# 1444-key attention: maxima as 32-row passes on quarters of the array, full-array products in front of the scores, three maxima in every key tile

## The reference

```python
qm, km, vm = (split_heads(t) for t in (q @ Wq.T + bq, k @ Wk.T + bk, v @ Wv.T + bv))
scores = einsum('bnlh,bnph->bnlp', qm, km) / sqrt(8)
scores = where(mask, scores, -1e8)
attn = softmax(scores, axis=-1)
out = einsum('bnlp,bnph->bnlh', attn, vm) @ Wo.T + bo
x = x + tanh(g_xattn[1]) * out
```

## Time and profile before

| what | value |
|---|---|
| median of 3 runs | 2146.14 us (2143.47 to 2155.18) |
| profiled execution, its own time | 2144.45 us |
| its span | 2142.7 us |
| mean granted clock of PE | 0.933 |
| PE busy | 89% of the span |
| VectorE, ScalarE, POOL busy | 69%, 62%, 31% |

### The profile page before, as it was taken

The page is one execution under the profiler, slowest core; times in us unless marked ns, Lnnn a source line. Parts: engine busy times, 40 slices in busy tenths (PEclk is TensorE's granted clock), DMA queues, the critical chain, the costliest instruction groups (busy, mean ns, idle before and its releaser), DMA issues. The chain is left out here.

```text
span 2142.7 us, 42902 instructions
## 1 busy us (share of the span) xinstructions
PE 1912.9 (89%) x16792; PEld 1207.6 (56%) x16792; DVE 1481.6 (69%) x3509; ACT 1323.4 (62%) x2169; POOL 670.7 (31%) x605
## 2 busy tenths in 40 slices
PE   3669999766899999999999999999999779999997
PEld 2536666544455656656565665656666445555553
DVE  4845666686677787877878787787884476677541
ACT  2645667677056766666676676766767355666643
POOL 1420233321421222322222222222210323565666
PEclk9879999867689999999999999999999597999998
DMA  5025555101232323323233232322322202212222
GB/s 159 1 68 176 186 168 186 36 20 39 85 120 74 133 83 111 115 83 133 77 117 106 92 132 67 127 96 101 129 77 67 63 15 47 50 36 36 36 71 43
DMA packets 126293, 190.74 MB, mean 89 GB/s; under 512 B 42018, under 2 KB 99466, under 8 KB 125710
## 3 DMA queue, kind: packets, MB, share of 16 engines
q1 hardware_dynamic: 126094, 188.01, 28.3%
HBM read 104.84 MB, written 11.76 MB: 54 GB/s over the span
## 5 line engine op out<-in xcount | busy, mean ns | idle before, releaser
L1608 DVE TENSOR_REDUCE b_part_max<-psum 128x1 f32<-128x482 f32 (+3 forms) x1248 | 741.7, 651 | 214.8 <-PE psum L1494 198.7
L1414 ACT ACTIVATE b_PT<-psum 128x800 f32<-128x800 f32 x768 | 608.2, 836 | 227.8 <-PE psum L1513 220.9
L1494 PE MATMUL psum<-b_KH,b_QBD 64*128 64x482 f32 (+1 forms) x1152 | 417.4, 438 | 21.2 <-DVE b_part_max L1608 18.5
L1513 PE MATMUL psum<-b_QS,b_KS 64*128 64x200 f32 x3072 | 420.4, 285 | 0.3 <-ACT b_PT L1414 0.3
L1513 PEld LDWEIGHTS psum<-b_QS,b_KS 64*128 64x128 f32 x3072 | 340.1, 187 | 5.7 <-ACT b_PT L1414 4.6
L1529 PE MATMUL psum<-b_PT,b_V 128*32 128x200 f32 x6144 | 341.5, 340 | 0.4 <-ACT b_PT L1414 0.4
L1339 POOL TENSOR_TENSOR b_KL<-b_KF,b_KH 128x1444 fp32r<-128x1444 f32 x32 | 107.0, 3342 | 589.0 <-PE psum L1513 565.7
L1494 PEld LDWEIGHTS psum<-b_KH,b_QBD 64*128 64x128 f32 x1152 | 194.2, 189 | 165.0 <-DVE b_part_max L1608 88.5
L1529 PEld LDWEIGHTS psum<-b_PT,b_V 128*32 128x32 f32 x6144 | 160.0, 109 | 144.1 <-ACT b_PT L1414 78.7
L1815 POOL TENSOR_TENSOR c_HE<-c_HE,c_G 128x400 f32<-128x400 f32 x128 | 131.6, 1032 | 115.1 <-ACT c_HE L1961 113.9
L426 POOL TENSOR_TENSOR a_rs<-a_ve,a_half 100x4 f32<-100x4 f32 x48 | 48.5, 1011 | 311.8 <-DVE a_ve L918 311.7
(11 more groups left out here) (280 smaller groups left out, 2996.2 us busy)
## 6 DMA issues: line engine op xcount, KB each, us to landing
b_KS<-b_KH SPq DMA_DIRECT2D x64, 722.0 KB
a_CT<-in_ctxt SPq DMA_DIRECT2D x32, 722.0 KB, 5.6
b_CT<-in_ctxt SPq DMA_DIRECT2D x32, 722.0 KB, 4.2
b_KS<-b_KL SPq DMA_DIRECT2D x32, 722.0 KB
a_CN<-in_ctxn SPq DMA_DIRECT2D x32, 704.0 KB
c_G<-gates_scratch SPq DMA_DIRECT2D x16, 800.0 KB, 4.3
att_scratch<-b_AO SPq DMA_DIRECT2D x32, 200.0 KB, 5.8
b_MB<-in_mask SPq DMA_DIRECT2D x32, 180.5 KB, 4.3
```

Source lines behind the costliest of these rows:

```text
L1414: nc.scalar.activation(PT[:, kt % 2, 2 * a:2 * a + 2, :], psum[:, 2 * a:2 * a + 2, 0:TG], ACT.Exp).then_inc(sem["pt_ready"], 1)
L1494: m = mm(bank(b, D, size), QBD[rows, j % 2, tile * D:(tile + 1) * D], KH[rows, j % 2, at_:at_ + size], start=True, stop=True)
L1513: m = mm(bank(p, D, 2 * T, (s % 2) * 2 * T), KS[rows, j % 2, s, kt * D:(kt + 1) * D], QS[rows, j % 2, s * 2 * T:(s + 1) * 2 * T], start=Tr ...
L1608: v.tensor_reduce(part_max[0:rows, n % 2, q, c:c + 1], bank(b, rows, CHUNKS[c][1]), AX.X, ALU.max)\
```

## The change

Each half of the array becomes two quarters of 32 rows. The columns of the projection weights are ordered so that a quarter holds four whole heads. `QBD` shrinks from 800 to 400 columns, and each quarter has 400 rows of maxima: three tiles of 128 and 16 left. A main maximum is now a pass of 32 rows by 128 columns, with the tile position given. The left-over rows of the four quarters are again one 64-column pass of 128 rows. The count of passes stays 36 + 3.

Each key tile has three maxima: one upper and two lower in even tiles, two upper and one lower in odd ones. Upper ones stand before score pieces 0 and 2, lower ones before piece 3, two in succession where there are two. Successive maxima of one half go to its two quarters in turn.

The jobs on the full array (query, key, value, left-over maxima) move from behind the scores to in front of them (`FRONT`); the turn stays behind (`BEHIND`). The left-over maxima stand in tiles 2, 6 and 7 instead of 5, 6 and 7, and the last main maximum is the last of all. The new order of rows asks for more transfers: 13 for `KS` and 10 for the maxima's rows of `QS`. ScalarE drains the values one tile earlier in its own order.

```diff
-TILES_ROW = 6
-LEFT = 32
-MAXES = 2 * TILES_ROW * 3 + 3
+QUARTERS, QROW, TILES_Q, LEFT = 4, 32, 3, 16
+MAXES = QUARTERS * TILES_Q * 3 + 3
-KS_DMAS = 4
+KS_DMAS, QROW_DMAS = 13, 10
-PHASES = 5
+FRONT, SCORES, BEHIND, PHASES = 0, 1, 5, 6
...
-MAIN_TILES = ((8, 1, 1), (9, 2, 2), (10, 2, 1), (11, 1, 2), (0, 2, 1), (1, 2, 2), (2, 1, 2), (3, 2, 1), (4, 1, 2), (5, 2, 1), (6, 1, 2),
-              (7, 1, 1))
+MAIN_TILES = tuple((kt, 1 + kt % 2, 2 - kt % 2) for kt in (8, 9, 10, 11, 0, 1, 2, 3, 4, 5, 6, 7))
+UPPER_AT, LOWER_AT = (0, 2), (3, 3)
+LEFT_TILES = (2, 6, 7)
...
     for kt, upper, lower in MAIN_TILES:
-        for p in list(range(upper)) + list(range(2, 2 + lower)):
-            half = 1 if p < 2 else 0
-            c, tile = divmod(used[half], TILES_ROW)
+        for half, p in [(1, p) for p in UPPER_AT[:upper]] + [(0, p) for p in LOWER_AT[:lower]]:
+            count, quarter = divmod(used[half], 2)
+            c, tile = divmod(count, TILES_Q)
             used[half] += 1
-            mains.append((half, tile, c, kt, p))
+            mains.append((2 * half + quarter, tile, c, kt, p))
...
-        jobs += [((g + 1, 0, "query", r), PHASES * kt + 4) for r, kt in QUERY_SLOTS[j]]
+        jobs += [((g + 1, 0, "query", r), PHASES * kt + FRONT) for r, kt in QUERY_SLOTS[j]]
     if nxt:
-        jobs += [((g, j + 1, "value", r), PHASES * (r + 2) + 4) for r in range(3)]
-        jobs += [((g, j + 1, "max", len(MAINS) + c), PHASES * (c + 5) + 4) for c in range(3)]
-        jobs.append(((g, j + 1, "turn", 0), PHASES * 8 + 4))
+        jobs += [((g, j + 1, "value", r), PHASES * (r + 2) + FRONT) for r in range(3)]
+        jobs += [((g, j + 1, "max", len(MAINS) + c), PHASES * kt + FRONT) for c, kt in enumerate(LEFT_TILES)]
+        jobs.append(((g, j + 1, "turn", 0), PHASES * 8 + BEHIND))
     if after:
-        jobs += [((g, j + 2, "key", r), PHASES * (r + 6) + 4) for r in range(3)]
+        jobs += [((g, j + 2, "key", r), PHASES * (r + 6) + FRONT) for r in range(3)]
...
-                    sp.dma_start(KS[r:D:4, j % 2, :, 0:S].bitcast(F32), part.bitcast(F32)).then_inc(t.ks_loaded[j % 2], 16)
+                    for quarter in range(QUARTERS):
+                        b, h = divmod(quarter, 2)
+                        sp.dma_start(KS[ROW * b + r:ROW * b + ROW:4, j % 2, 2 * h:2 * h + 2, 0:S].bitcast(F32),
+                                     part[QROW * quarter:QROW * quarter + QROW].bitcast(F32)).then_inc(t.ks_loaded[j % 2], 16)
...
+                    for quarter in range(QUARTERS):
+                        b, h = divmod(quarter, 2)
+                        sp.dma_start(quarters[b:b + 1, h, 0:TILES_Q * D],
+                                     part[TILES_Q * quarter:TILES_Q * (quarter + 1), :].bitcast(F32))\
+                            .then_inc(t.qrow_loaded[j % 2], 16)
+                    sp.dma_start(quarters[:, :, TILES_Q * D:], part[QUARTERS * TILES_Q:QCH, 0:QUARTERS * LEFT].bitcast(F32))\
+                        .then_inc(t.qrow_loaded[j % 2], 16)
...
-                        rows = slice(ROW * half, ROW * half + ROW)
+                        rows = slice(QROW * quarter, QROW * quarter + QROW)
                         m = mm(bank(b, D, size), QBD[rows, j % 2, tile * D:(tile + 1) * D], KH[rows, j % 2, at_:at_ + size],
-                               start=True, stop=True)
+                               start=True, stop=True, tile_position=(QROW * quarter, 0))
...
+                        some(PHASES * kt + FRONT)
                         for p in range(4):
-                            some(PHASES * kt + p)
+                            some(PHASES * kt + SCORES + p)
                             if not last or ahead[0] < GROUP:
                                 score_piece(g, *ahead, p)
-                        some(PHASES * kt + 4)
+                        some(PHASES * kt + BEHIND)
                         weigh(g, j, kt)
...
-    row_dims = np.concatenate([ROW * b + 2 * HD * (r % 4) + r // 4 for b in range(2)])
+    row_dims = np.concatenate([ROW * b + 2 * HD * (r // QROW * 2 + r % 2) + r % QROW // 2 for b in range(2)])
```

More of the change, by code:

```diff
@@ L1096 @@
 EARLY = sum(kt > 7 for _, _, _, kt, _ in MAINS)
+LAST_MAIN = len(MAINS) - 1
 def max_tile(i):
@@ L1102, in max_tile @@
         return MAINS[i][0:3]
[L1103 removed]
+    return None, QUARTERS * TILES_Q, i - len(MAINS)
 def ring_jobs(g, j, last):
@@ L1129, in first_ring_jobs @@
     jobs = [(0, 0, "query", r) for r in range(Q_JOBS)] + [(0, 0, "key", r) for r in range(3)]
-    for i in range(MAXES):
+    for i in list(range(LAST_MAIN)) + list(range(len(MAINS), MAXES)) + [LAST_MAIN]:
         jobs.append((0, 0, "max", i))
-        if i % 12 == 3 and i < len(MAINS):
+        if i % 12 == 3 and i < LAST_MAIN:
             jobs.append((0, 0, "value", i // 12))
@@ L1250, in stack_maxima @@
                     rows = slice(MAX_ROW + 4 * r, MAX_ROW + 4 * r + ROW + 1, ROW)
-                    sp.dma_start(QS[rows, j % 2, 0:TILES_ROW * D].bitcast(F32),
-                                 part[0:2 * TILES_ROW, :].bitcast(F32)).then_inc(t.qrow_loaded[j % 2], 16)
-                    sp.dma_start(QS[rows, j % 2, TILES_ROW * D:].bitcast(F32),
-                                 part[2 * TILES_ROW:QCH, 0:2 * LEFT].bitcast(F32)).then_inc(t.qrow_loaded[j % 2], 16)
+                    quarters = QS[rows, j % 2, :].bitcast(F32).rearrange("b (h c) -> b h c", h=2)
+                    for quarter in range(QUARTERS):
[5 more added lines that the diff above has]
+                        .then_inc(t.qrow_loaded[j % 2], 16)
             def store(g, j):
@@ L1483, in job @@
                 elif kind == "max":
-                    half, tile, c = max_tile(i)
+                    quarter, tile, c = max_tile(i)
                     if tile == 0:
@@ L1489, in job @@
                     at_, size = CHUNKS[c]
-                    if half is None:
-                        m = mm(bank(b, 2 * LEFT, size), QBL[:, j % 2, :], KH[:, j % 2, at_:at_ + size], start=True, stop=True)
+                    if quarter is None:
+                        m = mm(bank(b, QUARTERS * LEFT, size), QBL[:, j % 2, :], KH[:, j % 2, at_:at_ + size], start=True, stop=True)
                     else:
-                        rows = slice(ROW * half, ROW * half + ROW)
+                        rows = slice(QROW * quarter, QROW * quarter + QROW)
                         m = mm(bank(b, D, size), QBD[rows, j % 2, tile * D:(tile + 1) * D], KH[rows, j % 2, at_:at_ + size],
-                               start=True, stop=True)
+                               start=True, stop=True, tile_position=(QROW * quarter, 0))
                 else:
@@ L1605, in drain @@
                 elif kind == "max":
-                    half, tile, c = max_tile(i)
-                    rows, q = (2 * LEFT, QCH - 1) if half is None else (D, TILES_ROW * half + tile)
+                    quarter, tile, c = max_tile(i)
+                    rows, q = (QUARTERS * LEFT, QCH - 1) if quarter is None else (D, TILES_Q * quarter + tile)
                     v.tensor_reduce(part_max[0:rows, n % 2, q, c:c + 1], bank(b, rows, CHUNKS[c][1]), AX.X, ALU.max)\
                         .then_inc(drained, 1)
-                    if i == MAXES - 1:
+                    if i == LAST_MAIN:
                         dve.wait_ge(drained, done)
@@ L1613, in drain @@
                 else:
-                    wait(dve, t.qrow_loaded[1 - p], (2 * g + (j - 1) // 2 + 1) * 64)
+                    wait(dve, t.qrow_loaded[1 - p], (2 * g + (j - 1) // 2 + 1) * 16 * QROW_DMAS)
                     dve.wait_ge(sem["qexp_ready"], n + 1)
```

35 lines of the change are left out of this document (18 added, 17 removed).

## The result

The change made the kernel slower: 3048.69 us median of 4 runs (3025.09 to 3064.36) against 2149.93 of 4 runs of the kernel before (2143.47 to 2155.18), a ratio of 1.419 with a 95% interval of 1.4133 to 1.4248. The direction was forecast, the size was not: 2563 us was predicted, with 2400 to 2700 around it. The profiled execution took 3047.59 us, its span is 3045.8, and its mean granted clock is 0.744 instead of 0.933.

A forecast was written before the change was run, and what follows sets the result against it. The prediction took PE's chain of score loads, mode change, weighing and mode change to bound each tile; 15.4 - 1.1 - 0.9 = +13.4 us a sequence, +415 us over 31 sequences plus 3 once, gave 2563 us, range 2400 to 2700.

The forecast's parts named there:

- The sum: Attention stage: 15.4 - 1.1 - 0.9 = +13.4 us a sequence, pitch 46.9, +415 us over 31 sequences, plus 3 once.
- rival 3: Attention stage: pauses between blocks bring PE to 1.2 GHz; 3260 us for all tiles, 2900 for half; chance 0.03.
- Full boundaries: Key tiles: each 32-row maximum pauses against 64-row scores on both sides; 0.18 to 0.20 us a boundary, +1.28 a tile.
- eight score loads: First part of a key tile before: loads 0.11 us apart, 8 x 0.11 + 0.20 = 1.08 us, maxima costing PE nothing.
- the lone pass of the earlier trace: Left-over rows' 482-column maximum before the key product: 0.39 us, read as the cost of one pass alone in its block.
- The order's gain: Attention stage: even threes remove 1.1 us and shorter ring waits 0.9 us, together 2.0 us a sequence.
- Even threes: Three maxima in every tile: no fourth waits for a PSUM bank, removing 2 x 0.54 = 1.1 us a sequence.
- shorter waits for the ring: Full-array products in front of scores: less waiting for the ring's PSUM banks behind maxima, 0.15 in six tiles, 0.9 us a sequence.
- The stall taken as nothing: PE's wait for ten QS transfers before a sequence's first scores: 0 to 0.7 us, at most 22 us in all.
- 1.0 us to land: Last QS transfer: landing time in the lower estimate, with 0.40 an issue, giving 6.4 us after the turn.
- POOL's and `KS`'s terms: POOL's spread of the queries halves; KS takes 13 transfers instead of 4, 7 us of SP; both cost nothing.
- The 3 us for the first sequence: First sequence: nothing covers the six extra QS issues, 6 x 0.56 = 3 us, once.

The follow-up runs named there:

- the variant with one block: The changed kernel with all three maxima of a tile in front of its first score piece, still 32-row passes; 2561.97 us, ratio 1.1934.
- The best order on the old layout: Kernel before with the new order, 64-row passes, four transfers, upper maxima at score pieces 0, 1, lower at 2, 3, next group's HT loaded earlier; 2142.23 us, ratio 0.9967.

## Why the prediction was right in direction and wrong in size

**The step that failed is the clock.** The sum took the granted clock of before, 1.00 in the stage, for the kernel after, and the argument that it would stay ("passes still stream in more than half of each tile") was the one line of rival 3. PE is busy 99% after and still has 56 to 66% of its time at the 1.2 GHz level. Rival 3 had the price: "for half of them 2900", and by the same working about 3000 for 62%, the share of the stage that after spends at the low clock, against 3049 measured; with 0.03 I gave it almost no chance, though the prologue row showed that a PE busy 19.99 of 20 us can stand at 0.50. The reason I gave there, pauses between the blocks, is not it either: with three 128-row passes in the same blocks the clock is 1.00, and with three 32-row passes 0.58. The runs show instead that 32-row passes between the scores bring the clock down while PE has no wait (62 of after's 69 falls), and that with 128 rows in the same places it falls only at waits. The clock cost after 515 us, where the sum had nothing; the boundaries with all else at full clock cost 375. The Trainium skill (TensorE: Matmul & The Clock Gate, What's actually happening) says that the clock follows how busy PE has been; here two kernels that are both busy 500 of 500 us were granted 0.58 and 1.00, so the busy time of the profile is not what decides.

**Full boundaries: right.** The load of a 32-row pass waits for 64-row passes and the other way round, and the blocks have the length that 0.20 us a boundary gives: score blocks of two and four take 0.40 and 0.62 us against 0.42 and 0.64; a lone maximum costs 0.40 to 0.41 against 0.40, and the odd tile 2.64 against 2.68. The even one takes 1.83 instead of 2.08, since its six score loads stand on both halves and run partly beside each other (0.52 for six). That term was 0.12 us a tile too large.

**Two readings behind the terms were wrong.** The prediction took eight score loads, 0.11 apart, as one chain that bounds a tile. With nothing between them they take 0.53 us together, as the variant with one block shows. In the tile of the earlier trace rows the second half's scores, which begin at 1002.74, had waited for ScalarE, whose second exponential ends at 1001.12 + 1.57 = 1002.69 (timelines before, of PE's weight loads and of ScalarE):

```profile
1002.74 0.18 PEld L1513 LDWEIGHTS psum<-b_QS,b_KS 64*128 64x128 f32 x1
```

```profile
1001.12 1.57 ACT L1414 ACTIVATE b_PT<-psum 128x800 f32<-128x800 f32 x2 [0.60 <-PE psum L1513]
```

In the last sequence of the earlier trace rows the second half's loads begin 0.05 us behind that exponential in all of the nine tiles. So ScalarE shares in those 1.10 us, and the equal tiles there do not show that PE alone bounds them. The other reading is the lone pass of the earlier trace rows: 0.39 us from the left-over maximum to the key product held a wait for VectorE of 0.25, as the row says, and after the same two loads start 0.06 us apart (1004.93 and 1004.99). It was no sample of a block between two changes of mode; as far as that row goes, it was luck that such a block does take 0.40 to 0.41; the sum 0.11 + 0.19 + 0.10 beside it was the better ground.

The rule of the Trainium skill that the prediction names (TensorEngine Tiling (Array Packing), Key Properties) agrees with the blocks of after, also for passes on different rows of the array.

**The order's gain: wrong, and small.** Even threes and shorter waits for the ring were to bring 2.0 us a sequence. The best order on the old layout brought 0.5, the new one nothing to be measured. This error of 1.5 us a sequence nearly cancels that of the even tiles, 12 x 0.12 = 1.4. At full clock a sequence took 45.5 us against the 46.9 predicted, which is close by that luck; the 1.4 left over are not traced.

**QS: the price was wrong, the conclusion held.** An issue takes 0.68 us in this row (6.8 for ten), not 0.56, and the first scores wait a further 1.07. After has few such waits, six of 1.7 us in 600 to 2540 us with no name and one of 3.9 on the DMA, at the last sequence, since its slow tiles cover them; in tiles of 1.9 us they cost 4.1 us each and the clock behind them. The stall taken as nothing was nothing mostly because the low clock stretched the tiles: the seven waits stand behind full-clock stretches, and the clock falls beside each. The prediction's 1.0 us to land had no row to it; 1.07 was measured.

**The rest: right.** POOL's and `KS`'s terms are nothing: two layouts with 4 and 13 transfers agree within 0.4%. Reductions stay at 0.65 us, weighing at 0.81. The 3 us for the first sequence did not appear: it starts 1.3 us earlier.

## What to carry to other kernels

Passes of different array shapes don't run beside each other even on different rows: a small pass hidden beside a larger one of its shape costs its whole time (0.4 us here) when it gets a shape of its own. Before cutting the rows of a pass, ask what the clock will do: a PE that was busy all the time, with 32-row passes between its scores, was at half the clock for 84% of it. A busy share near 100% says nothing of that; the granted clock has to be read beside it. And a transfer split into many is paid at its issuer: before, the four issues end at 1034.1 and the scores that need them start at 1037.07, so there were about 2 us of slack (an estimate, with the 1.07 from issue to scores above), and in the new order six more issues made PE wait 4.1 us.

## What was not expected of the hardware

- In a stretch where PE was never idle the granted clock was 0.58 with three 32-row maxima and 1.00 with three 128-row ones in the same places; one maximum of 32 rows instead of three: 0.72; score passes doubled: 0.72.
- One wait of 4.1 us a sequence of 40 us (301 exponentials in 500 us) went with a clock of 0.89 in a kernel that had 0.98 with four transfers in place of ten. A wait of 1.2 us was enough for a fall in the variant with single 128-row maxima. How the wait's length and the passes around it share in that stays open.
- Three 32-row maxima in one block ahead of the scores brought no fall without a wait; the same passes spread between the scores did. Why the place matters stays open.
- Left-over maxima of 64 columns and key products of 128 start 0.06 us apart (1004.93, 1004.99 above): this change of columns, from 64 to 128 with all rows in use, does not pause, nor does that of the earlier trace rows; the one from 128 to 36 in the earlier trace rows does.
